# Stacked query and key parts loaded as long rows, the maxima's band copied heads outermost, and expert units moved to other places of the schedule

## The chip, the cores and the metric

The kernel runs on one core of one Trainium2 chip. The metric is the device time of one launch in microseconds (us), the median of several runs. The core has five engines that run their own instruction streams and meet in semaphores: TensorE (PE, with its weight loads shown as PEld), VectorE (DVE), ScalarE (ACT), GpSimd (POOL) and SyncE (SP), whose queue issues the DMAs here. Sixteen DMA engines move the bytes.

## The reference, cut to what matters

Eight samples go through one block, one after the other: a token mixer and a text embedding give 384 rows of 256, then attention with relative positions, then eight gated experts.

```python
h = concat([L0_tok(x), W_E[x_txt] * sqrt(256)], axis=1)      # (8, 384, 256)
# attention: 16 heads of 16, band of 9 relative positions (|s - t| <= 4)
q = (ln(h) @ Wq + bq) * 0.25;  k = ln(h) @ Wk + bk;  v = ln(h) @ Wv + bv
w = q @ k.T + rel_to_abs(q @ rel_k.T)                          # per head, 384 x 384
p = softmax(w)
h = h + (p @ v + abs_to_rel(p) @ rel_v) @ Wo + bo
# experts: e_out = (silu(x @ Wg) * (x @ Wu)) @ Wd per expert, weighted by a router
h = h + einsum('bte,betd->btd', weights(ln(h)), e_out)
```

## The kernel before, in words

**Staging.** `rounds` gives every engine the same list of steps from `schedule`: one round with attention of sample 0 alone, a loop of seven rounds (`Fori(1, NB)`) with attention of sample b and the experts of sample b - 1, and a last one with the experts of sample 7. An engine does of each step what its own block defines, so the order of steps is fixed by hand.

**Expert units.** The experts of a sample are 48 units of TensorE work: per expert two `gate`, two `up` (six matmuls of 384 columns each, in split precision) and `down` parts 0 and 1 (eight and four recorded matmuls). Each is followed by work of DVE (`hidden`, `accumulate`) or ACT (`silu`). `fill(n)` puts the next n units behind a step. The tables FILL_MIX, FILL_MAXIMA, FILL_NEGATE and FILL_OUT say how many: before, 31 units lie in the mixer and projections, 20 of them after `project_v`, 5 between the maxima, 2 after `negate` and 10 in the output part.

**Queries and keys.** `project_qk` computes q and k transposed: two blocks of 128 columns (m = 0, 1), partition = column within the block, 384 rows along the free axis. Each is split into three bf16 parts, `parts[0..5]`. SP writes each part to HBM (`part_out`, L533), in rows of 768 bytes of `d_parts[n]`, and `stack` (L538) reads them back, six DMAs for `q_st` and six for `k_st`: each fills 16 partitions (the 16 columns of a head) with 16 heads of 384 bf16. Six such groups of 16 partitions stand above each other, so one matmul over the partitions adds the products of the parts. Both `part_out` and `stack` write or read 192 KB per DMA.

**The band.** `project_rel` computes the relative logits; SP writes them askew to `d_band_t` (L549), reads the band back into `band_t` (L567, 128 partitions, bf16, window outer and head inner), and does the same in float32 for `bands` (L571, L580). All of these stand in SP's queue in this order: parts, `q_st` zero rows (L559), six loads of `q_st`, six of `k_st`, the load of `band_t`, three writes of `d_band_s`, two loads of `bands`.

**Maxima.** 24 items per sample, each of two tiles of 128 rows: a matmul `q_st` by `k_st` of 384 columns (L746), and one of the identity by `band_t[rows, i, w0:w1, h]` of 132 or 136 columns (L754), which reads one element in 16. Two pairs of PSUM banks take turns. DVE reduces both tiles of an item at once (`maxima`, L1168). Item 0 waits for all stacks and for `band_t`; item n waits for the reduction of item n - 2. After 12 and 24 items `negate` turns the maxima and SP takes them through HBM to rows 96 and 97 of `q_st`. Then `attend` computes scores anew, DVE adds `bands` (L1189), ACT takes exp (L999), POOL cuts windows (L1432).

**Start.** SP issues 9, 4 and 30 small loads (groups 0 to 2, L473), the zeroing of three HBM tensors (L493 to L504), then the first expert weights (L509). `prepare` (DVE, L1118 to L1131) waits for all of group 2, stands behind the sums of sample 0's mixer in DVE's order, and makes `rel_k` and others; ACT's and TensorE's first `project_qk` wait for the semaphore `consts`.

## Time and profile before

| | |
|---|---|
| median of 3 runs | 1387.92 us (1380.27 to 1393.97) |
| the profiled execution | 1391.63 us, span 1389.6 us |
| busy: PE, PEld, DVE | 1160.2, 811.2, 751.2 us |
| busy: ACT, POOL | 370.3, 234.4 us |
| granted TensorE clock, mean | 0.907 of full speed |
| DMA | 89.59 MB, mean 64 GB/s |

The span is the time from the first to the last instruction that the profile shows. Busy time is the sum over an engine's instructions, so an engine can be 83% busy and still be waited for only in parts. One round of the loop takes some 161 us. The stages below are those of the third round, whose stacks are issued from 389.5 us.

### The profile page before, as it was taken

What the parts mean: (1) busy time and instruction counts of PE and PEld (TensorE: products, weight loads), DVE (VectorE), ACT (ScalarE), POOL (GpSimd) and SP (SyncE); (2) the same over time, 40 slices, a digit from 0 to 9 for tenths busy, and PEclk for the clock granted to TensorE, in tenths of its full rate; (3) what the DMA queues carried; (4) which work ended last, traced back from release to release, by engine and by line L of the source; (5) the groups of instructions that cost most, each with busy time, mean ns of one, the idle gap of its engine ahead of it and who ended that gap; (6) DMA issues with size and microseconds to landing.
All of it is one profiled execution on the core that took longest, in us unless ns stands there. A gap on an engine that the chain in (4) does not pass through costs nothing.

```text
span 1389.6 us, 16995 instructions
## 1 busy us (share of the span) xinstructions
PE 1160.2 (83%) x5732; PEld 811.2 (58%) x5732; DVE 751.2 (54%) x1579; ACT 370.3 (27%) x599; POOL 234.4 (17%) x258
## 2 busy tenths in 40 slices
PE   5447699878898898988899788987889888997798
PEld 4212378426784377735785267843777357852588
DVE  6337264763548545573556635475455735466333
ACT  1214212062222522043220622115120432206111
POOL 5404120040200302022200402004020212004000
PEclk9667789988899989999899989999899998999889
DMA  6691207302092102901055020921029010650200
GB/s 210 159 199 62 43 5 128 86 1 59 0 161 52 35 23 57 155 1 35 23 96 116 5 54 0 162 51 35 23 51 160 1 35 23 100 112 1 46 0 12
DMA packets 126985, 89.59 MB, mean 64 GB/s; under 512 B 67991, under 2 KB 116504, under 8 KB 126522
## 3 DMA queue, kind: packets, MB, share of 16 engines
q1 hardware_dynamic: 126552, 88.05, 31.4%
q0 software_dynamic: 384, 1.05, 0.3%
q14 instruction: 38, 0.31, 0.1%
q8 instruction: 11, 0.18, 0.1%
HBM read 60.36 MB, written 28.71 MB: 64 GB/s over the span
## 4 chain that ended last, share of the span: by engine, by line
PE 31%; issue 28%; DVE 15%; DMA 12%; SPq 5%; ACT 5%; POOL 2%; POOLq 0%; DVEq 0%; ACTq 0%
DMA scratch<-d_band_t 9%; PE S L881 7%; PE S L754 4%; PE S L902 4%; DVE S L1189 4%; PE S L746 4%; SPq L538 4%; PE S L809 4%; ACT scratch L999 3%; DVE maxima L1168 3%; PE S L710 3%; PE S L794 2%; DMA txt_row<-in_L_txt_W_E,txt_idx 1%; PE S L627 1%; DMA w_d<-in_L_ffn_Wu 1%
## 5 line engine op out<-in xcount | busy, mean ns | idle before, releaser
L1168 DVE TENSOR_REDUCE maxima<-S 128x2 f32<-128x768 f32 x192 | 176.0, 953 | 82.1 <-PE S L754 80.6
L1432 POOL TENSOR_TENSOR bands<-scratch,one 64x432 f32<-64x432 f32 x128 | 119.5, 934 | 585.8 <-ACT scratch L999 580.7
L902 PE MATMUL S<-w_d,hT 128*128 128x256 f32 x768 | 198.6, 412 | 8.1 <-DVE hT L1306 8.1
L902 PEld LDWEIGHTS S<-w_d,hT 128*128 128x128 f32 x768 | 158.6, 210 | 34.1 <-issue 10.8
L746 PE MATMUL S<-k_st,q_st 128*128 128x384 bf16 x384 | 137.1, 357 | 49.1 <-DMA scratch<-d_band_t 34.7
L1189 DVE TENSOR_TENSOR S<-S,bands 64x144 f32<-64x144 f32 x384 | 154.3, 402 | 43.9 <-PE S L794 34.2
L999 ACT ACTIVATE scratch<-S 128x768 f32<-128x768 f32 x192 | 155.6, 811 | 56.5 <-DVE S L1189 49.1
L1037 ACT ACTIVATE silu<-S 128x384 f32<-128x384 f32 x128 | 62.9, 491 | 396.4 <-PE S L881 309.9
L754 PE MATMUL S<-scratch,ident_b 128*128 128x132 bf16 (+1 forms) x384 | 154.5, 402 | 0.0
L1306 DVE TENSOR_TENSOR hT<-silu,S 128x384 f32<-128x384 f32 x128 | 70.6, 552 | 117.9 <-PE S L881 115.7
L794 PE MATMUL S<-q_st,k_st 128*128 128x384 bf16 x384 | 93.2, 342 | 36.4 <-ACT scratch L999 34.8
L809 PE MATMUL S<-scratch,v_one 128*17 128x384 f32 x768 | 90.9, 569 | 27.5 <-ACT scratch L999 27.4
L746 PEld LDWEIGHTS S<-k_st,q_st 128*128 128x128 bf16 x384 | 38.5, 100 | 117.1 <-DVE maxima L1168 58.8
L1318 DVE SCALAR_TENSOR_TENSOR res<-S,wgt,res 128x256 f32<-128x256 f32 x168 | 75.5, 479 | 50.0 <-PE S L902 49.6
L794 PEld LDWEIGHTS S<-q_st,k_st 128*128 128x128 bf16 x384 | 25.6, 99 | 121.8 <-ACT scratch L999 92.5
L881 PE MATMUL S<-x_hi,wu_hi 128*128 128x384 f32 x256 | 75.5, 377 | 14.3 <-DVE hT L1306 14.0
L881 PE MATMUL S<-x_hi,wg_hi 128*128 128x384 f32 x256 | 80.3, 396 | 0.0
L627 PE MATMUL S<-ident,scratch 128*128 128x128 f32 x196 | 35.6, 330 | 52.0 <-DVE scratch L1079 30.1
L1349 POOL TENSOR_TENSOR rstd<-mv,eps 128x3 f32<-128x3 f32 (+1 forms) x24 | 4.6, 193 | 387.1 <-DVE mv L1073 387.1
L881 PE MATMUL S<-x_hi,wu_lo 128*128 128x384 f32 x256 | 68.3, 349 | 0.0
L881 PE MATMUL S<-x_lo,wu_hi 128*128 128x384 f32 x256 | 68.3, 349 | 0.0
L881 PE MATMUL S<-x_lo,wg_hi 128*128 128x384 f32 x256 | 67.2, 344 | 0.0
(159 smaller groups left out, 1578.4 us busy)
## 6 DMA issues: line engine op xcount, KB each, us to landing
bands<-d_band_s SPq DMA_DIRECT2D x16, 864.0 KB, 8.8
scratch<-d_band_t SPq DMA_DIRECT2D x8, 1632.0 KB, 16.9
d_parts<-scratch SPq DMA_DIRECT2D x48, 192.0 KB, 2.0
q_st<-d_parts SPq DMA_DIRECT2D x48, 192.0 KB
k_st<-d_parts SPq DMA_DIRECT2D x48, 192.0 KB
d_band_w<-bands SPq DMA_DIRECT2D x32, 240.0 KB, 3.8
out<-scratch SPq DMA_DIRECT2D x8, 384.0 KB, 2.7
x_in<-in_x SPq DMA_DIRECT2D x8, 256.0 KB, 3.7
```

Of the source, the lines that this page charges most:

```text
L746: pe.matmul(S[:, bank, PAD:PAD + T], q_st[:, h, i * P:(i + 1) * P], k_st[:, h, :], start=True, stop=False, skip_group_check=True)
L754: mm = pe.matmul(S[rows, bank, at + w0:at + w1], ident_b[rows, rows], band_t[rows, i, w0:w1, h], start=False, stop=True, skip_group_check= ...
L794: mm = pe.matmul(S[:, 2 * (n % 3) + l, PAD:PAD + T], k_st[:, h, i * P:(i + 1) * P], q_st[:, h, :], start=True, stop=True)
L809: mm = pe.matmul(S[32 * l:32 * l + VC, 6 + g % 2, 0:T], v_one[:, i, h, :], p_t[:, h % PTS, i, :], start=(i == 0), stop=(i == TT - 1), skip ...
L881: mm = pe.matmul(dst[:, 0:T], ws[:, e, k, m * P:(m + 1) * P], xs[:, k, :], start=(j == 0), stop=(j == 3 * KT - 1))
L902: mm = pe.matmul(D[:, i // 2, (i % 2) * E:(i % 2 + 1) * E], hT[:, (FT * e + m) % 3, i * P:(i + 1) * P], w_d[:, e, m, :], start=(m == 0), s ...
L999: nc.scalar.activation(dst, S[:, c0:c0 + 2, PAD:PAD + T], ACT.Exp).then_inc(exp_done.sem, 1)
L1168: dve.tensor_reduce(dst, S[:, c0:c0 + 2, PAD:PAD + T], AX, ALU.max).then_inc(max_done.sem, 1)
L1189: dve.tensor_tensor(win, win, band, ALU.add).then_inc(sc_add.sem, 1)
L1306: dve.tensor_tensor(hT[:, n % 3], silu[:], U[:, 0:T], ALU.mult).then_inc(h_done.sem, 1)
L1318: dve.scalar_tensor_tensor((out_st if last else res)[:, i], D[:, i // 2, (i % 2) * E:(i % 2 + 1) * E], wgt[:, i, e:e + 1], res[:, i], ALU. ...
L1432: nc.gpsimd.tensor_tensor(bands[rows, :, :, 2 * pair:2 * pair + 2].rearrange("p i w h -> p h i w"), win, one[rows].unsqueeze(2).unsqueeze( ...
```

## The change

The columns of Wq and Wk, and their biases, are reordered on chip so that a partition holds (d, group of heads) rather than (head, d). A part is then written to HBM as it lies on chip, in rows of 1536 bytes, and a stack DMA reads for each of its 16 partitions one run of 12,288 bytes. ScalarE copies `band_t` two heads at a time into `band_h`, heads outermost, and the identity matmuls read 132 neighbouring elements. The biases and `emb_rel_k` are loaded by 16 small DMAs each. The unit tables are changed: `project_v` 20 to 9, maxima 5 to 12, `negate` 2 to 3, output part 10 to 13.

```diff
...
 EPS = 1e-5
 ITEMS = AH * TT // 2
 WINS = P // BL
-N_LOADS = (9, 4, 13 + P // AD + NJ)
+N_LOADS = (9, 4, 10 + 3 * AD + NJ)
 N_ZERO = 8
-N_CONSTS = 8
+N_CONSTS = 12
 FILL_MIX = [("residual", 0), ("mix_in", 0), ("turn_x2", 0), ("mix_sums", 0), ("router", 1),
             ("mix_out", 0), ("router_zone", 1), ("mix_norm", 1), ("router_rank", 2),
             ("norm_stats", 2), ("router_pick", 1), ("turn_norm", 2), ("project_qk", 0),
-            ("project_rel", 1), ("project_v", 20)]
-FILL_MAXIMA = [0, 0, 0, 1, 0, 0, 0, 1, 0, 0, 0, 1, 0, 0, 0, 1, 0, 0, 0, 1, 0, 0, 0, 0]
-FILL_NEGATE = 2
-FILL_OUT = [("turn_outputs", 6), ("turn_weights", 2), ("rel_values", 2), ("turn_attn", 0)]
+            ("project_rel", 1), ("project_v", 9)]
+FILL_MAXIMA = [0, 1] * 12
+FILL_NEGATE = 3
+FILL_OUT = [("turn_outputs", 7), ("turn_weights", 2), ("rel_values", 3), ("turn_attn", 1)]
 R_DIST = 4
 ZONE_LO = float(np.float32(0.5 - np.log(4.0 / 3.0)))
 ZONE_HI = 0.5
...
         ident = sb("ident", [P, P])
         ident_b = sb("ident_b", [P, P], BF16)
-        head_of_row = sb("head_of_row", [P, KT, AH])
         head_of_rel = sb("head_of_rel", [P, AH])
         earlier = sb("earlier", [P, NE, NE])
         wkv = sb("wkv", [F + 1, 2 * F])
...
         emb_k_rows = zone(7640, NJ)
+        row_head, w_in = zone(7700, AH // KT), zone(6528, 2, KT, E)
         emb_v_rows0, emb_v_rows1 = zone(7656, AD), zone(7672, AD)
         rel_log_b = Z[:, 4272:4272 + TT * RJ // 2].bitcast(BF16).rearrange("p (i r) -> p i r", i=TT)
         BAND_AT = ZF - TT * ROWB // 2
         band_t = Z[:, BAND_AT:ZF].bitcast(BF16).rearrange("p (i w h) -> p i w h", i=TT, h=AH)
+        band_h = Z[:, 0:TT * ROWB // 2].bitcast(BF16).rearrange("p (i h w) -> p i h w", i=TT, h=AH)
+
...
         REL_TILES = ((0, S[:, 0, 0:E]), (1, S[:, 2, 0:E]), (2, O[:, 0:E]))
-        d_parts = nc.dram_tensor("d_parts", [6, E, T], BF16, kind="Internal").ap()
+        d_parts = nc.dram_tensor("d_parts", [6, P, KT, T], BF16, kind="Internal").ap()
         d_zero = nc.dram_tensor("d_zero", [2, AH, T], BF16, kind="Internal").ap()
         d_neg = nc.dram_tensor("d_neg", [2, 2, AH // 2, T], BF16, kind="Internal").ap()
         d_band_t = nc.dram_tensor("d_band_t", [T * ROWB], BF16, kind="Internal").ap()
...
         mask_float, wb_masked, ew_exp = sem("mask_float"), sem("wb_masked"), sem("ew_exp")
         ew_turned, ew_ready, resid_ready = sem("ew_turned"), sem("ew_ready"), sem("resid_ready")
         temp_inverse, wr_high, consts = sem("temp_inverse"), sem("wr_high"), sem("consts")
+        row_mask = sem("row_mask")
         gu_high, gu_low, pool_consts = sem("gu_high"), sem("gu_low"), sem("pool_consts")
         x_loaded = sig("x_loaded", 1, 16)
         idx_loaded = sig("idx_loaded", 1, 16)
...
         stacked = sig("stacked", 2 * SLOTS + 1, 16)
         rel_t_out, rel_s_out = sig("rel_t_out", P // BT, 16), sig("rel_s_out", TT, 16)
         band_t_in, band_s_in = sig("band_t_in", 1, 16), sig("band_s_in", WINS, 16)
+        band_turned = sig("band_turned", AH // 2)
         max_pe = sig("max_pe", ITEMS)
         max_done = sig("max_done", ITEMS)
         neg_pe, neg_act, neg_dve = sig("neg_pe", 2), sig("neg_act", 2), sig("neg_dve", 2)
...
                 (ln_g[:], a["L0_tok_ln_g"].partition_broadcast(P)),
                 (ln_b[:], a["L0_tok_ln_b"].partition_broadcast(P)),
             ], [
-                (head_of_row[:], a["head_of_row"]), (head_of_rel[:], a["head_of_rel"]),
+                (head_of_rel[:], a["head_of_rel"]),
                 (earlier[:], a["earlier"]),
-                (bq4[:], a["L0_attn_bq"].rearrange("(k p) -> p k", p=P)),
-                (bk1[:], a["L0_attn_bk"].rearrange("(k p) -> p k", p=P)),
-                (w_q[:], a["L0_attn_Wq"].rearrange("(k p) n -> p k n", p=P)),
-                (w_k[:], a["L0_attn_Wk"].rearrange("(k p) n -> p k n", p=P)),
+                (w_in[:, 0], a["L0_attn_Wq"].rearrange("(k p) n -> p k n", p=P)),
+                (w_in[:, 1], a["L0_attn_Wk"].rearrange("(k p) n -> p k n", p=P)),
                 (w_v[:], a["L0_attn_Wv"].rearrange("(k p) n -> p k n", p=P)),
                 (w_o[:], a["L0_attn_Wo"].rearrange("(k p) n -> p k n", p=P)),
                 (bv_all[:], a["L0_attn_bv"].partition_broadcast(P)),
...
             ]]
             emb_v = a["L0_attn_emb_rel_v"]
-            for r in range(P // AD):
-                groups[2].append((emb_k_rows[AD * r:AD * (r + 1)],
-                                  a["L0_attn_emb_rel_k"].rearrange("o j d -> d (o j)")))
+            G8 = P // AD
+            for d in range(AD):
+                rows = slice(d * G8, (d + 1) * G8)
+                groups[2] += [
+                    (emb_k_rows[rows], dram(a["L0_attn_emb_rel_k"], d, (0, G8), (AD, NJ))),
+                    (bq4[rows], dram(a["L0_attn_bq"], d, (KT * AD, G8), (AD, KT))),
+                    (bk1[rows], dram(a["L0_attn_bk"], d, (KT * AD, G8), (AD, KT)))]
             for j in range(NJ):
                 rows = slice(AH * j, AH * (j + 1)) if j < P // AH else slice(0, AH)
                 at = emb_v_rows0 if j < P // AH else emb_v_rows1
...
                 def part_out(n, done, k, out):
                     sp.wait_ge(done.sem, done.at(b, k))
-                    sp.dma_start(d_parts[n].rearrange("(m p) t -> p m t", p=P), parts[n]
+                    sp.dma_start(d_parts[n], parts[n]
                                  ).then_inc(out.sem, 16)
                 def stack(st, base, order):
                     for n in range(SLOTS):
                         sp.dma_start(
-                            st[AD * n:AD * (n + 1)],
-                            d_parts[base + order[n]].rearrange("(h d) t -> d h t", d=AD)
+                            st[AD * n:AD * (n + 1)].rearrange("p h t -> p (h t)"),
+                            d_parts[base + order[n]].rearrange("(d g) m t -> d (g m t)", d=AD)
                         ).then_inc(stacked.sem, 16)
                 part_out(0, proj_act, 3, q_out)
...
                     if not later(b):
                         pe.wait_ge(pool_consts, 8)
                     pe.wait_ge(stacked.sem, stacked.at(b, 2 * SLOTS + 1))
-                    pe.wait_ge(band_t_in.sem, band_t_in.at(b, 1))
-
                     pe.wait_ge(v_done.sem, v_done.at(b, TT))
                     pe.wait_ge(proj_act.sem, proj_act.at(b, 9))
+                if n % 3 == 0:
+                    pe.wait_ge(band_turned.sem, band_turned.at(b, n // 3 + 1))
                 if n >= 2:
                     pe.wait_ge(max_done.sem, max_done.at(b, n - 1))
                 for l, (h, i) in enumerate(tiles_of(n)):
...
                         w0, w1 = (WIN if first else 0), (WB - WIN if last else WB)
                         at = PAD + i * P + c * BT - WIN
                         mm = pe.matmul(S[rows, bank, at + w0:at + w1], ident_b[rows, rows],
-                                       band_t[rows, i, w0:w1, h],
+                                       band_h[rows, i, h, w0:w1],
                                        start=False, stop=True, skip_group_check=True)
                 mm.then_inc(max_pe.sem, 1)
...
                 act.wait_ge(proj_act.sem, proj_act.at(b, 9))
                 nc.scalar.activation(rel_log_b, rel_log, ACT.Copy).then_inc(proj_act.sem, 1)
+            def maxima(b, n):
+
+                if n == 0:
+                    act.wait_ge(band_t_in.sem, band_t_in.at(b, 1))
+                ahead = {0: (0, 1), ITEMS - 3: ()}
+                for pair in ahead.get(n, (n // 3 + 1,) if n % 3 == 0 else ()):
+                    heads = slice(2 * pair, 2 * pair + 2)
+                    nc.scalar.activation(band_h[:, :, heads], band_t[:, :, :, heads].rearrange("p i w h -> p i h w"),
+                                         ACT.Copy).then_inc(band_turned.sem, 1)
+
             def weights(b):
                 for n in range(4):
...
                 nc.scalar.activation(silu[:], G[:, 0:T], ACT.Silu).then_inc(silu_done.sem, 1)
             rounds(act, {"mix_in": mix_in, "prepare": prepare, "turn_norm": turn_norm,
-                         "project_qk": project_qk, "project_rel": project_rel, "weights": weights,
+                         "project_qk": project_qk, "project_rel": project_rel, "maxima": maxima, "weights": weights,
                          "negate": negate, "attend": attend, "copy": copy, "turn_weights": turn_weights,
                          "turn_attn": turn_attn, "turn_x2": turn_x2, "router": router, "gate": gate})
...
             def prepare(b):
                 dve.wait_ge(loaded[2], 16 * N_LOADS[2])
+                dve.tensor_tensor(row_head, head_of_rel[:, 0:AH // KT], head_of_rel[:, AH // KT:AH], ALU.add
+                                  ).then_inc(row_mask, 1)
+                dve.memset(rel_k[:], 0.0).then_inc(row_mask, 1)
+                dve.wait_ge(row_mask, 2)
                 for m in range(KT):
-                    dve.tensor_tensor(rel_k[:, m], emb_k_rows.unsqueeze(2).broadcast_to([P, NJ, AH]),
-                                      head_of_row[:, m].unsqueeze(1).broadcast_to([P, NJ, AH]), ALU.mult
+                    dve.tensor_tensor(rel_k[:, m].rearrange("p j (g m) -> p m j g", m=KT)[:, m],
+                                      emb_k_rows.unsqueeze(2).broadcast_to([P, NJ, AH // KT]),
+                                      row_head.unsqueeze(1).broadcast_to([P, NJ, AH // KT]), ALU.mult
                                       ).then_inc(consts, 1)
+                for n, w in enumerate((w_q, w_k)):
+                    for k in range(KT):
+                        dve.tensor_copy(w[:, k].rearrange("p (m d g) -> p m d g", m=KT, d=AD),
+                                        w_in[:, n, k].rearrange("p (g m d) -> p m d g", m=KT, d=AD)
+                                        ).then_inc(consts, 1)
                 for dst, rows, n in ((rel_v0, emb_v_rows0, P), (rel_v1, emb_v_rows1, RJ - P)):
                     dve.tensor_tensor(dst[:], rows[0:n].unsqueeze(1).broadcast_to([n, AH, AD]),
                                       head_of_rel[0:n].unsqueeze(2).broadcast_to([n, AH, AD]), ALU.mult
```

## Rows read from the trace of the kernel before

**Rows 1.** The page's chain that ended last, by line

```profile
DMA scratch<-d_band_t 9%; PE S L881 7%; PE S L754 4%; PE S L902 4%; DVE S L1189 4%; PE S L746 4%; SPq L538 4%; PE S L809 4%; ACT scratch L999 3%; DVE maxima L1168 3%; PE S L710 3%; PE S L794 2%; DMA txt_row<-in_L_txt_W_E,txt_idx 1%; PE S L627 1%; DMA w_d<-in_L_ffn_Wu 1%
```

**Rows 2.** The same chain in order of time: start, us, what

```profile
388.63 0.36 SPq L533
...
396.87 16.91 DMA scratch<-d_band_t
...
422.52 1.05 PE S L881 x6
...
443.22 2.59 PE S L902 x12
```

**Rows 3.** Windows of transfers: engines' busy time, clock, DMA share, GB/s

```profile
387.50:388.00 0.50, 0.50 (x4) 0.45 (x3) 0.47 (x2) 0.00 (x0) 0.00 (x0) 1.00 1.00 307
392.00:409.00 17.00, 17.00 (x92) 16.26 (x91) 6.25 (x13) 2.46 (x5) 0.00 (x0) 1.00 1.16 131
393.25:393.50 0.25, 0.25 (x3) 0.25 (x2) 0.25 (x2) 0.00 (x0) 0.00 (x0) 1.00 1.12 108
394.00:394.25 0.25, 0.25 (x3) 0.25 (x2) 0.00 (x0) 0.00 (x0) 0.00 (x0) 1.00 1.40 191
...
395.50:395.75 0.25, 0.25 (x3) 0.25 (x3) 0.25 (x1) 0.00 (x0) 0.00 (x0) 1.00 1.35 194
410.50:412.00 1.50, 1.50 (x10) 1.37 (x9) 0.55 (x1) 0.02 (x1) 0.00 (x0) 1.00 1.04 418
474.50:476.50 2.00, 1.39 (x13) 0.55 (x6) 0.00 (x0) 1.07 (x2) 0.00 (x0) 0.84 1.01 200
420.00:422.00 2.00, 1.76 (x10) 0.60 (x8) 1.79 (x3) 0.00 (x0) 0.00 (x0) 1.00 1.03 200
```

**Rows 4.** TensorE in order of time, before and after its wait

```profile
399.67 0.71 PE L881 MATMUL S<-x_hi,wg_hi 128*128 128x384 f32 x2
...
414.09 0.33 PE L746 MATMUL S<-k_st,q_st 128*128 128x384 bf16 x1 [1.32 <-DMA scratch<-d_band_t]
...
414.26 0.40 PE L754 MATMUL S<-scratch,ident_b 128*128 128x132 bf16 x1
...
414.48 0.34 PE L746 MATMUL S<-k_st,q_st 128*128 128x384 bf16 x1
```

**Rows 5.** The same window view of the maxima stage and of the output part

```profile
414.09:442.70 28.61, 26.28 (x127) 13.96 (x127) 23.92 (x30) 1.46 (x3) 0.00 (x0) 1.00 0.33 66
...
475.35:498.26 22.91, 19.91 (x96) 16.12 (x97) 7.74 (x19) 5.09 (x10) 0.00 (x0) 0.93 0.25 44
```

**Rows 6.** Groups by line in one maxima stage: busy us, mean ns, idle before

```profile
L1168 DVE TENSOR_REDUCE maxima<-S 128x2 f32<-128x768 f32 x24 | 21.9, 952 | 7.1 <-PE S L754 7.1
```

**Rows 7.** Groups by line over the whole span

```profile
L1318 DVE SCALAR_TENSOR_TENSOR res<-S,wgt,res 128x256 f32<-128x256 f32 x168 | 75.5, 479 | 50.0 <-PE S L902 49.6
L1306 DVE TENSOR_TENSOR hT<-silu,S 128x384 f32<-128x384 f32 x128 | 70.6, 552 | 117.9 <-PE S L881 115.7 <-DVE scratch L1279 1.3
...
L959 ACT ACTIVATE scratch<-scratch 128x768 bf16<-128x768 f32 x16 | 13.5, 843 | 0.5
```

**Rows 8.** Windows of the clock, the first round's and a later one's

```profile
63.00:84.00 21.00, 0.03 (x1) 0.06 (x2) 0.00 (x0) 0.00 (x0) 5.84 (x2) 0.50 1.14 185
84.00:92.50 8.50, 8.50 (x30) 3.25 (x31) 6.07 (x7) 0.00 (x0) 0.00 (x0) 0.50 0.70 129
...
471.50:475.25 3.75, 3.73 (x24) 0.94 (x24) 0.00 (x0) 0.00 (x0) 1.87 (x2) 0.54 0.25 52
```

**Rows 9.** Loads at the start, and who waits for them

```profile
18.38 4.13 SPq L473 DMA_DIRECT2D scratch<-in_L_attn_emb_rel_v  x9
...
23.67 0.20 ACT L937 ACTIVATE bq<-bq 128x2 f32<-128x2 f32 x1 [6.44 <-DMA scratch<-in_L_attn_emb_rel_v]
...
36.81 0.51 DVE L1118 TENSOR_TENSOR rel_k<-scratch,head_of_row 128x144 f32<-128x144 f32 x2
```


## The prediction

> **What bounds the kernel now.** I read the page first. Its chain by line gives the wait for `scratch<-d_band_t`, the load of the maxima's band, the largest share, 9% [rows 1]. The chain in order of time says why: the last part leaves at 388.63, the twelve stacks follow, the load of `band_t` is issued at 396.87 and takes 16.91 us although it is one DMA [rows 2]. It stands behind the stacks in the same rings. In the windows the stacks fill the time from 392 to 409 at 131 GB/s, and the band itself then runs at 418 [rows 3]. TensorE works through its 20 units meanwhile and idles 1.32 us before item 0 at 414.09 [rows 4]. So before this point two things are nearly equal: 20 units of TensorE's work, and the stacks. In the maxima stage (28.61 us) PE is busy 26.28 and DVE 23.92 us [rows 5]; in the output part PE is busy 19.91 of 22.91 us [rows 5]. TensorE's work is the bound of the loop, and moving units pays only where the place they leave shrinks by as much.
>
> **Do longer rows make the stacks faster?** This decides the sum. Within one stack the windows show a plateau of 108 GB/s, with a peak of 191 to 194 each time the next stack begins, at 394.0 and again at 395.5 [rows 3]: one stack in 1.5 us, twelve in 18. Parts are written from 128 partitions in the same 768-byte rows at 307 GB/s, so that row length is not what holds the stacks at a third of this. Transfers with long rows but fewer partitions are slow too: the loads of `bands` (64 partitions, rows of 4608 bytes) run at 200 GB/s, the stores of windows (32 partitions each, rows of 2560 bytes) at 200, `band_t` on 128 partitions at 418 [rows 3]. The rate follows the partitions that a transfer spans, and a stack still spans 16. I therefore take 1.5 us for a stack as before. Bounds: 1.8 us, if the peaks at the seams vanish (196,608 bytes at 108 GB/s), and 1.25 us, if the seams grow to twice their share; for twelve that is +3.7 and -3.0 us a round.
>
> The Trainium skill, SBUF — State Buffer, section "Door 1: The DMA port swizzle", speaks against this change: 16 partitions reach 4 of 16 ports, and it gives 104 GB/s for a 1 MiB transfer on partitions 0 to 15, whose rows are long. The trace agrees within a stack (108 GB/s). By the page's figure a stack would take an estimated 1.89 us, and the sum would be some 37 us higher over eight rounds.
>
> **Units leaving `project_v`.** Nine units instead of 20 follow `project_v`. In the trace the ninth ends at 399.64, where the next gate begins at 399.67 [rows 4]. With the stacks as slow as before the band still lands at 413.8, so PE idles some 15 us there: nothing is gained.
>
> **The copy to `band_h`.** PE no longer waits for the load but for ACT's copy of the first head pair: 3*2*136 = 816 elements. ACT copies 768 to bf16 in 0.843 us [rows 7], so 0.90 us, plus a semaphore: item 0 starts 1.1 us later (0.9 to 2.0, if reading one element in 16 doubles it). The other seven copies run ahead on an ACT that is busy 1.46 of 28.61 us [rows 5]; what queues behind them is `silu`, with slack. Cost zero.
>
> **The maxima stage.** Now a tile is a matmul of 384 columns and one of the identity. They start 0.17 and 0.22 us apart (414.09, 414.26, 414.48 [rows 4]): the short one takes longer than the long one. With neighbouring elements it should take between its share at the other's rate (0.06) and no gain (0.22); I take 0.10, near the long one's rate but with a weight load of its own. An item is then 2*(0.18+0.10) = 0.56 us of PE instead of 0.80. A gate or up takes 1.05 us, both down parts together 2.59 [rows 2], so a unit is (4*1.05+2.59)/6 = 1.13 us. Two items and their unit: 1.12+1.13 = 2.25 us. DVE: 21.9/24 = 0.91 us an item [rows 6], and per six units two `hidden` (0.55) and three `accumulate` (0.48) [rows 7], 0.42 a unit: 1.82+0.42 = 2.24. Both engines are full; twelve such pairs take 27.0, and the transposes, the last reduction and semaphores 1.6: 28.6 us at full clock, as now, with seven units more. That is what the contiguous band buys: 24*0.24 = 5.8 us of PE, about five units.
>
> But the stage now starts after 15 us of idle. In the first round PE idles from 63 to 84 and the granted clock is 0.50; it stays there for 8.5 us of work, 84.0 to 92.5, and in a later place for 3.75 us of dense work [rows 8]. The maxima with units are dense, so nearer the second: 5 us at 1.2 instead of 2.4 GHz, 2.5 us lost (1.9 to 4.3). The stage takes 31.1 us: +2.5.
>
> **Units arriving elsewhere.** `negate` holds gate, up, gate (3*1.05) instead of both down parts (2.59): +0.6. The output part gets three units more, up and both down parts: 1.05+2.59 = 3.6 us. PE idles 22.91-19.91 = 3.0 us there now [rows 5], in the waits for the output's copies, the windows' way through HBM and the expert tail; I count 2.3 of it as filled (a unit behind a wait fills it, one that overshoots delays the chain): +1.3. Together +1.9 a round (0.9 to 3.5).
>
> **The start.** Group 2 grows from 30 loads to 10+48+9 = 67. Nine small ones are issued in 4.13 us [rows 9], 0.46 each, so 37 more take 17.0 us on SP, ahead of the zeroing and the expert weights. The last load ends its issue at 22.5 and ACT passes at 23.67 [rows 9]; now at 40.7. DVE reaches `prepare` at 36.81 [rows 9], so 13 of the 17 us are hidden by the first mixer and 3.9 are not. DVE adds a mask sum, a memset and four copies of 256 columns, each at most the 0.48 of an `accumulate` of that width: 2.1 us, all in the chain that leads to the first norm. Start: +6.0 (4.5 to 8).
>
> **The sum.** Seven rounds of the loop: 7*(0+1.1+2.5+1.9) = 38.5. First round: no units; its end waits for expert weights whose loads stand in SP's queue behind the band, so neither copy nor item counts: 0. Start 6.0. Last round unchanged. 1391.63+44.5 = 1436; against the median, 3.7 us below the profiled execution, **1432 us**. Its own range: stacks -24 to +30, clock -4 to +13, identity matmul up to +30 (no gain) or -5, the rest -10 to +15: these hardly come together, 1400 to 1475.
>
> **Rivals.**
> (a) *Long rows do free the stacks.* If 768-byte reads, not the 16 partitions, set 131 GB/s, a stack takes 0.47 to 0.64 us (196,608 bytes at 418 or 307 GB/s [rows 3]), and twelve some 7 instead of 18: 11 us less. The band lands near 402.8, three to four us after the ninth unit. A round changes by -11+1.1+0+1.9 = -8.0 with hardly any clock lost: -56, first round and start -11+6: 1326 to 1335, **1329 us**. For it: no other transfer here reads 768-byte rows from HBM into 16 partitions, and the mean of 131 GB/s lies above the plateau. Against: the plateau itself and the 32- and 64-partition rows. It is faster from the point where a round saves more than the 5.5 us it costs plus its share of the start, at stacks under 0.96 us.
> (b) *Engines run on.* With one run of 12,288 bytes per engine and stack, engines that finish early write the next stack's partitions, and the 194 GB/s of the seams [rows 3] becomes the mean: 1.01 us a stack, -5.9 a round. Then 7*(-5.9+5.5) = -3, first round and start about 0: **1385 us**, no change.
> (c) *The identity matmul gains nothing.* 0.22 as before: PE 2.73 us per pair of items, +5.8 a round more on the forecast, 1472. It lies in the forecast's range.
>
> **Chances.** Forecast with (c) 0.64, (b) 0.12, (a) 0.24. Under 1% (14 us) this kernel's runs hardly tell from no change. Slower by more: 0.60, from the forecast less its low tail; within 1%: 0.14; faster: 0.26, (a) and a part of (b). Range: the forecast's own up to 1475, (b), and half of (a): 1332 to 1475.
>
> **What would show it.** Right: windows of the stacks again near 108 GB/s within one and 1.5 us apart; PE idle some 15 us before item 0 and clock 0.50 in the first microseconds of the maxima; short matmuls under 0.12 us apart; `prepare` waiting for a load near 40 us. Wrong: a band load that lands under 10 us after its issue and stacks over 250 GB/s. The forecast falls with its first step, the rate of a stack; everything else in it is worth some 10 us.

## The result, and the profile after

The changed kernel takes 1471.62 us (median of 4 runs, 1469.70 to 1473.85) beside 1390.16 us for the kernel before on the same chip (4 runs). The ratio is 1.0618, with a 95% interval of 1.0572 to 1.0663: 81 us slower. The profiled execution took 1469.7 us, its span is 1467.9 us against 1389.6 before, +78.3.

The page of the changed kernel, its busy times and the chain by line:

```profile
span 1467.9 us, 17186 instructions
...
PE 1086.0 (74%) x5732; PEld 786.7 (54%) x5732; DVE 747.9 (51%) x1585; ACT 473.1 (32%) x663; POOL 234.1 (16%) x258
...
DMA scratch<-d_band_t 9%; PE S L887 7%; DVE maxima L1194 4%; PE S L908 3%; PE S L815 3%; ACT scratch L1015 3%; DVE S L1215 3%; SPq L479 3%; PE S L716 3%; SPq L544 3%; ACT scratch L985 3%; PE S L800 2%; PE S L752 2%; PE S L633 1%; DMA txt_row<-in_L_txt_W_E,txt_idx 1%
...
L985 ACT ACTIVATE scratch<-scratch 128x816 bf16<-128x816 bf16 x64 | 106.3, 1703 | 121.5 <-DMA scratch<-d_band_t 121.5
```

TensorE has 74 us less to do (1160.2 before) and the kernel is longer all the same. The band's load still leads the chain [rows 1]; two lines are new on it, SP's small loads (L479) and ACT's copies (L985), 3% each.

**Where the 78.3 us lie.** A round begins for this count when SP issues its first part (`part_out`). The marks, from SP's queue in order of time, split the span:

| stretch | before, us | after, us | difference | forecast |
|---|---|---|---|---|
| start to the first part | 54.37 | 69.57 | +15.2 | +6.0 |
| first part of round 0 to that of round 1 | 161.84 | 173.96 | +12.1 | 0 |
| the next six, mean of one | 162.8 | 170.8 | +8.0, six times | +5.5 |
| from the last such mark to the end | 196.7 | 199.7 | +3.0 | +5.5 |

15.2 + 12.1 + 6*8.0 + 3.0 = 78.3. Single rounds scatter: the six of the kernel before lie between 160.1 and 167.2 us (the third round's 161 among them), those after between 170.2 and 171.9. The 8.0 lie far outside this scatter, while one or two us between the means of two kernels may be scatter.

**The start.** SP's loads and DVE's first steps behind them, in order of time (start, us, what, and the idle time before it with its releaser):

```profile
23.32 0.68 SPq L479 DMA_DIRECT2D bq<-in_L_attn_bq  x1
24.04 0.67 SPq L479 DMA_DIRECT2D bk<-in_L_attn_bk  x1
24.75 0.46 SPq L479 DMA_DIRECT2D scratch<-in_L_attn_emb_rel_k  x1
...
44.53 4.03 SPq L479 DMA_DIRECT2D scratch<-in_L_attn_emb_rel_v  x9
...
49.66 0.17 DVE L1133 TENSOR_TENSOR scratch<-head_of_rel 128x8 f32<-128x8 f32 x1 [12.77 <-DMA scratch<-in_L_attn_emb_rel_v]
49.83 0.30 DVE L1135 MEMSET rel_k<- 128x288 f32 x1
...
50.46 0.65 DVE L1144 COPY w_q<-scratch 128x256 f32<-128x256 f32 x2
51.03 0.65 DVE L1144 COPY w_k<-scratch 128x256 f32<-128x256 f32 x2
```

The pattern of three loads repeats 16 times. A load of `emb_rel_k` costs 0.46 us, as the small loads did before [rows 9], but each slice of a bias costs 0.68, or 0.72 from one issue to the next. The nine loads of `emb_rel_v` end at 48.56 instead of 22.51, and DVE waits 12.77 us for them.

**The first round.** ACT, TensorE and DVE in order of time:

```profile
117.34 1.91 ACT L993 ACTIVATE wu_hi<-w_d 128x2048 fp32r<-128x2048 f32 x1 [40.25 <-DMA w_d<-in_L_ffn_Wu]
120.28 1.91 ACT L993 ACTIVATE wu_hi<-w_d 128x2048 fp32r<-128x2048 f32 x1 [1.03 <-DMA w_d<-in_L_ffn_Wu]
122.09 9.53 ACT L985 ACTIVATE scratch<-scratch 128x816 bf16<-128x816 bf16 x6
123.90 0.48 PE L752 MATMUL S<-k_st,q_st 128*128 128x384 bf16 x1 [48.98 <-ACT scratch L985]
...
124.96 1.82 DVE L1194 TENSOR_REDUCE maxima<-S 128x2 f32<-128x768 f32 x2 [49.03 <-PE S L760]
```

ACT takes its steps in program order. The cast of the expert weights (`weights`, before `maxima` in the schedule) waits 40.25 us for the load of `Wu`, and the new copies stand behind it. Item 0 of the maxima starts at 123.90; before, it started at 84.0 [rows 8], since it needed no step of ACT behind the cast. Counted from the round's own first part, that is 54.3 us instead of 29.6.

**The stage that the forecast reads, third round.** The chain in order of time:

```profile
425.33 20.11 DMA scratch<-d_band_t
445.46 1.67 ACT scratch L985
447.18 0.50 PE S L752
...
456.27 1.76 ACT scratch L985
458.15 0.33 PE S L752
```

SP's queue there, in order of time:

```profile
417.96 1.31 SPq L539 DMA_DIRECT2D d_parts<-scratch  x2
419.42 0.25 SPq L565 DMA_DIRECT2D q_st<-d_zero  x1
419.80 2.63 SPq L544 DMA_DIRECT2D q_st<-d_parts  x6
422.48 2.73 SPq L544 DMA_DIRECT2D k_st<-d_parts  x6
425.33 0.38 SPq L573 DMA_DIRECT2D scratch<-d_band_t  x1
```

Windows of the same stage, columns as in [rows 3]:

```profile
421.50:439.50 18.00, 8.84 (x46) 7.94 (x44) 3.41 (x8) 0.98 (x2) 0.00 (x0) 0.84 1.03 121
430.00:433.00 3.00, 0.34 (x2) 0.00 (x0) 0.39 (x1) 0.00 (x0) 0.00 (x0) 1.00 0.94 111
447.18:479.66 32.48, 28.25 (x171) 20.70 (x171) 26.78 (x36) 13.69 (x12) 0.00 (x0) 0.94 0.27 55
447.18:451.00 3.82, 3.82 (x15) 2.86 (x16) 2.21 (x3) 1.51 (x1) 0.00 (x0) 0.53 0.45 94
451.00:452.00 1.00, 1.00 (x11) 0.77 (x9) 0.48 (x1) 0.94 (x2) 0.00 (x0) 1.00 1.01 203
```

The stacks with their rows of 12,288 bytes run at 121 GB/s, where those of 768 bytes ran at 131 [rows 3]. The load of the band lands 20.11 us after its issue (16.91 before [rows 2]) and 26.5 us after the last part was ready; before it was 25.1. TensorE has done its nine units long before; its instructions in order of time:

```profile
447.18 0.50 PE L752 MATMUL S<-k_st,q_st 128*128 128x384 bf16 x1 [16.84 <-ACT scratch L985]
447.48 0.32 PE L760 MATMUL S<-scratch,ident_b 128*128 128x132 bf16 x1
447.59 0.53 PE L752 MATMUL S<-k_st,q_st 128*128 128x384 bf16 x1
...
451.04 0.22 PE L760 MATMUL S<-scratch,ident_b 128*128 128x132 bf16 x1
451.10 0.33 PE L752 MATMUL S<-k_st,q_st 128*128 128x384 bf16 x1
```

It idles 16.84 us and runs at half clock until 451 (0.53), then at full. At full clock a long matmul (384 columns) follows a short one (the identity's, 132 columns) after 0.06 us (451.04 to 451.10), where it took 0.22 us before [rows 4]. The maxima stage takes 32.48 us (28.61 before [rows 5]). At its end the turn of the maxima has to wait for DVE's three `accumulate` steps of the unit just ahead of it (they read the PSUM bank that it writes); DVE and TensorE in order of time:

```profile
478.35 1.26 DVE L1344 SCALAR_TENSOR_TENSOR res<-S,wgt,res 128x256 f32<-128x256 f32 x3
479.66 0.49 PE L633 MATMUL S<-ident,maxima 128*8 128x128 f32 x3 [1.73 <-DVE res L1344]
```

### The profile page after: what moved, and what is told of

Same layout as the page of the kernel before. It is cut to its first block, busy times and chain, and to the rows that moved or that the text cites. A ratio compares the mean times of both kernels' runs of the same rounds, so it can differ in the third digit from the quotient of the medians.

```text
span 1467.9 us, 17186 instructions
## 1 busy us (share of the span) xinstructions
PE 1086.0 (74%) x5732; PEld 786.7 (54%) x5732; DVE 747.9 (51%) x1585; ACT 473.1 (32%) x663; POOL 234.1 (16%) x258
## 4 chain that ended last, share of the span: by engine, by line
issue 30%; PE 24%; DVE 15%; DMA 13%; ACT 8%; SPq 7%; POOL 2%; POOLq 0%; DVEq 0%; ACTq 0%
DMA scratch<-d_band_t 9%; PE S L887 7%; DVE maxima L1194 4%; PE S L908 3%; PE S L815 3%; ACT scratch L1015 3%; DVE S L1215 3%; SPq L479 3%; PE S L716 3%; SPq L544 3%; ACT scratch L985 3%; PE S L800 2%; PE S L752 2%; PE S L633 1%; DMA txt_row<-in_L_txt_W_E,txt_idx 1%
## 5 line engine op out<-in xcount | busy, mean ns | idle before, releaser
L752 PE MATMUL S<-k_st,q_st 128*128 128x384 bf16 x384 | 108.7, 349 | 175.0 <-ACT scratch L985 166.5
L908 PE MATMUL S<-w_d,hT 128*128 128x256 f32 x768 | 181.9, 382 | 6.2 <-DVE hT L1332 6.2
L908 PEld LDWEIGHTS S<-w_d,hT 128*128 128x128 f32 x768 | 141.3, 190 | 26.1 <-issue 7.6
L985 ACT ACTIVATE scratch<-scratch 128x816 bf16<-128x816 bf16 x64 | 106.3, 1703 | 121.5 <-DMA scratch<-d_band_t 121.5
L815 PE MATMUL S<-scratch,v_one 128*17 128x384 f32 x768 | 85.7, 536 | 25.6 <-ACT scratch L1015 25.2
L760 PE MATMUL S<-scratch,ident_b 128*128 128x132 bf16 (+1 forms) x384 | 88.8, 232 | 0.0
L887 PE MATMUL S<-x_lo,wg_hi 128*128 128x384 f32 x256 | 71.2, 362 | 0.0
L633 PEld LDWEIGHTS S<-ident,scratch 128*128 128x128 f32 x196 | 27.9, 169 | 78.2 <-DVE scratch L1095 53.8
L887 PE MATMUL S<-x_hi,wg_lo 128*128 128x384 f32 x256 | 69.6, 355 | 0.0
```

The costliest lines, as they stand in the source:

```text
L633: return pe.transpose(dst, src, ident[0:rows, 0:rows])
L752: pe.matmul(S[:, bank, PAD:PAD + T], q_st[:, h, i * P:(i + 1) * P], k_st[:, h, :], start=True, stop=False, skip_group_check=True)
L760: mm = pe.matmul(S[rows, bank, at + w0:at + w1], ident_b[rows, rows], band_h[rows, i, h, w0:w1], start=False, stop=True, skip_group_check= ...
L815: mm = pe.matmul(S[32 * l:32 * l + VC, 6 + g % 2, 0:T], v_one[:, i, h, :], p_t[:, h % PTS, i, :], start=(i == 0), stop=(i == TT - 1), skip ...
L887: mm = pe.matmul(dst[:, 0:T], ws[:, e, k, m * P:(m + 1) * P], xs[:, k, :], start=(j == 0), stop=(j == 3 * KT - 1))
L908: mm = pe.matmul(D[:, i // 2, (i % 2) * E:(i % 2 + 1) * E], hT[:, (FT * e + m) % 3, i * P:(i + 1) * P], w_d[:, e, m, :], start=(m == 0), s ...
```

## The experiments

Theory A is the forecast's, with the three costs that the trace of the changed kernel added to it: slow stacks on 16 partitions with an empty TensorE above them, SP's many small loads, and ACT's order in round 0. Its rivals are named in the expectations. The kernel before ran on each chip too, at medians of 1383.0 (the first four experiments), 1385.2 (the next four) and 1387.5 us (the last four), so kernels are compared by their ratios, and by the marks of their traces. "A round" below is the mean of the six stretches between marks. In the diffs "..." stands for lines left out.

### The unit tables of before (e1_old_tables)

```diff
-            ("project_rel", 1), ("project_v", 9)]
-FILL_MAXIMA = [0, 1] * 12
-FILL_NEGATE = 3
-FILL_OUT = [("turn_outputs", 7), ("turn_weights", 2), ("rel_values", 3), ("turn_attn", 1)]
+            ("project_rel", 1), ("project_v", 20)]
+FILL_MAXIMA = [0, 0, 0, 1, 0, 0, 0, 1, 0, 0, 0, 1, 0, 0, 0, 1, 0, 0, 0, 1, 0, 0, 0, 0]
+FILL_NEGATE = 2
+FILL_OUT = [("turn_outputs", 6), ("turn_weights", 2), ("rel_values", 2), ("turn_attn", 0)]
```

> The changed kernel with the four unit tables of the kernel before. Theory A (the stacks are as slow as before, so the 11 units left a hole in which TensorE idles and its clock falls): the hole closes, the maxima stage is bound by VectorE with only 5 units in it (24*0.91 plus 2.0 plus 1.5 = 25.4 us instead of 32.5), later stages give 2 us back, the band lands as before: a round loses 9 us, 7*9 = 63, about 1408 us. Rival B (the copies to band_h, 1.70 us each, hold the round up wherever the units are): a round loses 3 us or less, 1450 us or more.

Measured: 1408.99 us, ratio 1.0165 (1.0111 to 1.0219). A round takes 161.0 us, 9.8 less than in the changed kernel. TensorE idles 2.17 us before item 0 of the third round instead of 16.84. So the places of the units make all of the loop's loss that can be told from the 162.8 before. The start and round 0 keep their losses (first parts at 69.64 and 245.36).

### One load for each of the three arrays (e2_few_loads)

```diff
-            for d in range(AD):
-                rows = slice(d * G8, (d + 1) * G8)
-                groups[2] += [
-                    (emb_k_rows[rows], dram(a["L0_attn_emb_rel_k"], d, (0, G8), (AD, NJ))),
-                    (bq4[rows], dram(a["L0_attn_bq"], d, (KT * AD, G8), (AD, KT))),
-                    (bk1[rows], dram(a["L0_attn_bk"], d, (KT * AD, G8), (AD, KT)))]
+            groups[2] += [(emb_k_rows, a["emb_k_rows"]), (bq4[:], a["bq_rows"]), (bk1[:], a["bk_rows"])]
...
```

The three arrays are laid out in rows on the host, before the launch.

> The changed kernel with the two biases and emb_rel_k laid out in rows beforehand and loaded by one DMA each, 3 instead of 48. Theory A (SP's issue of the small loads holds up the first projections): project_qk of the first round moves from 62.5 us to 50 or less, 13 to 15 us off the whole, 1457 us. Rival B (the first round ends with the expert weights in any case, so a later start is absorbed): no change, 1471 us.

Measured: 1456.33 us, ratio 1.0526 (1.0496 to 1.0557). The first part leaves at 56.66 us instead of 69.57: 12.9 of the start's 15.2 us are the 45 loads. Of the 2.3 us that stay, DVE's added steps in `prepare` are 1.5 (it takes 3.1 us instead of 1.6), and the first projection takes 0.8 more: its eight matmuls by `w_q` take 5.46 us, all in a stretch at half clock, and took 4.68, the last part of them at full clock.

### Round 0's copies ahead of the cast of Wu (e3_copies_first)

```diff
             def maxima(b, n):
+                if not later(b):
+                    return
...
                 for n in range(4):
+                    if n == 2:
+                        act.wait_ge(band_t_in.sem, band_t_in.at(b, 1))
+                        for pair in range(AH // 2):
+                            heads = slice(2 * pair, 2 * pair + 2)
+                            nc.scalar.activation(band_h[:, :, heads], ...
```

> The changed kernel with ScalarE's eight copies of the first round ahead of its casts of the Wu halves, instead of behind them. Theory A (in the first round the maxima wait for copies queued behind casts that wait for weights): the maxima start about 105 instead of 124 us and end before the weights are ready; attend follows the landing of Wu by 18 instead of 28 us, 10 us off, 1461 us. Rival B (SP's negate stands behind the weights, so the maxima's place does not matter): no change, 1471 us.

Measured: 1458.05 us, ratio 1.0534 (1.0504 to 1.0565). ACT and TensorE in order of time, round 0:

```profile
101.48 12.59 ACT L996 ACTIVATE scratch<-scratch 128x816 bf16<-128x816 bf16 x8 [24.46 <-DMA scratch<-d_band_t]
103.29 0.48 PE L752 MATMUL S<-k_st,q_st 128*128 128x384 bf16 x1 [29.06 <-ACT scratch L996]
...
118.11 1.91 ACT L1001 ACTIVATE wu_hi<-w_d 128x2048 fp32r<-128x2048 f32 x1 [4.04 <-DMA w_d<-in_L_ffn_Wu]
```

The same copies, the same wait for the band, and in round 0 only the order changed: item 0 starts 20 us earlier, the cast still finds its data late (4.04 us), and round 0 takes 162.0 us, as before the change. So this order makes the 12.1 us of round 0.

### The strided read kept, no copy (e4_no_copy)

```diff
-                if n % 3 == 0:
-                    pe.wait_ge(band_turned.sem, band_turned.at(b, n // 3 + 1))
...
-                                       band_h[rows, i, h, w0:w1],
+                                       band_t[rows, i, w0:w1, h],
...
```

TensorE waits for the band's load again, and ACT's copies are taken out.

> The changed kernel without the copies: the identity matmuls read one element in 16 of band_t again, with the new tables. Theory A (the contiguous band makes room on TensorE, the copy costs a start and the first round): start of the maxima 1.7 us earlier, two items and a unit 2.73 instead of 2.25 us of TensorE, stage 34.5 instead of 32.5 us, first round 10 us less: 7*0.3-10, about 1463 us. Rival B (the copies are the main cost of a round): 3 us or more off each round, 1440 us or less. Rival C (TensorE is the bound of the stage): 5 us or more on each, 1495 us or more.

Measured: 1482.16 us, ratio 1.0701 (1.0670 to 1.0732), between theory A and rival C: the loss in a round is ten times what A gave. Round 0 gets 12.4 us shorter, the other rounds 3.4 us longer each (174.2). Groups by line: the identity's matmuls are back at their length of before.

```profile
L759 PE MATMUL S<-scratch,ident_b 128*128 128x132 bf16 (+1 forms) x384 | 154.8, 403 | 0.0
```

So with 12 units between the maxima the contiguous band is worth 3.4 us a round net of its copy. It is the part of the change that earns something. Counted from item 0 to the last reduction the stage takes 36.0 us here and 31.2 with `band_h`, 4.8 us of the 5.8 of TensorE that the prediction worked out; the first copy takes 1.4 of them back.

### The three fixes together (e5_three_fixes)

Old tables, few loads and copies first, in one kernel; the long rows and the contiguous band stay.

> The changed kernel with old unit tables, few start loads and the first round's copies ahead of the casts, together. Theory A (the three losses lie in different stretches and add up): 1471.6-62.6-15.3-13.6 = 1380 us, level with the kernel before or up to 1% faster, since long rows and band_h cost and gain little by themselves. Rival B (they overlap: the first round waits for the expert weights in any case): 1395 us or more.

Measured: 1383.17 us (10 runs), ratio 0.9986 (0.9949 to 1.0024). The three costs add up, and what is left of the change, as a whole, is worth nothing that can be told. A round takes 161.5 us (162.8 before). That hides two effects of opposite sign, which e8 below separates.

### One load on 96 partitions for each stack (e6_wide)

`part_out` writes a part once for every slot that uses it, into `d_stack`, and one DMA per stack reads all six slots. Its rows have the same 12,288 bytes and all loads together move the same bytes; one spans 96 partitions instead of 16, and there are two instead of twelve.

```diff
-                    for n in range(SLOTS):
-                        sp.dma_start(
-                            st[AD * n:AD * (n + 1)].rearrange("p h t -> p (h t)"),
-                            d_parts[base + order[n]].rearrange("(d g) m t -> d (g m t)", d=AD)
-                        ).then_inc(stacked.sem, 16)
+                    sp.dma_start(
+                        st[0:KST].rearrange("p h t -> p (h t)"),
+                        d_stack[base // 3].rearrange("s (d g) m t -> (s d) (g m t)", d=AD)
+                    ).then_inc(stacked.sem, 16)
...
```

> The changed kernel, but each part is written to HBM once for each slot that uses it, and q_st and k_st are each loaded by one DMA over 96 partitions instead of six over 16; rows of 12,288 bytes and all bytes read stay the same, written bytes double. Theory A (a stack's rate goes by the partitions that a transfer spans): the two loads take 4 to 5 us each instead of 18 together, the band lands 9 us earlier in each of 8 rounds, 72 us off, 1400 us. Rival B (something else holds the stacks at 131 GB/s, the reading side for one): no gain, 1475 us with the additional writes.

Measured: 1420.48 us, ratio 1.0229 (1.0155 to 1.0303). Windows of the stacks in the third round:

```profile
413.00:415.00 2.00, 2.00 (x11) 1.77 (x10) 0.88 (x3) 0.00 (x0) 0.00 (x0) 1.00 1.03 255
415.00:417.00 2.00, 2.00 (x13) 2.00 (x12) 0.58 (x2) 0.49 (x1) 0.00 (x0) 1.00 1.02 258
```

The chain in order of time behind them:

```profile
414.02 14.95 DMA scratch<-d_band_t
429.00 1.67 ACT scratch L986
430.71 0.50 PE S L753
```

The rate doubles. It is not the number of loads that held it down: in both traces the DMA engines are busy all through (DMA share 1.03 here, and 1.03 at 121 GB/s above), and a packet of 12,288 bytes takes 0.81 us instead of 1.56 in the mean of the 194 of this stage. That the loads also read other places of HBM was not tried by itself. From the issue of the first stack (412.20) to the landing of the band it takes 16.8 us instead of 25.6, nearly the 9 us less that were expected. The size fell short all the same, 54 us by the ratios and 49 by the spans where 72 were expected. In the mean of six rounds it is 17.1 instead of 24.8 us, and the first stack is issued 1.0 us later, behind six more writes of parts. So the band lands 6.7 us earlier after a round's first part, and a round gives back 7.0 us (163.8). Round 0 gives back 2.6 only, as its item 0 still stands behind the cast of `Wu`. The Trainium skill, SBUF — State Buffer, section "Door 1: The DMA port swizzle", lets the rate follow the ports that the partitions of one transfer reach. The runs agree: 16 partitions stay at 121 to 131 GB/s with either row, 96 give 255.

### The same with the start and round 0 mended (e7_wide_fixes)

e6 with few loads and copies first.

> The same 96-partition loads with few start loads and the first round's copies ahead of the casts, new unit tables. Theory A: the gains of those two fixes (15.3 and 13.6 us) add to the wide loads' 72: 1371 us, faster than the kernel before. Rival B (without the slow stacks in front, the first round's end is set by the expert weights alone, and the fixes there no longer count in full): 1385 us.

Measured: 1391.10 us (10 runs), ratio 1.0027 (0.9999 to 1.0055). Against e6 that is 29 us less, both mends in full; the miss against the expectation (1371 us) is e6's. A round still takes 163.7 us, with 9.5 us of idle ahead of item 0 in the third: nine units are too few even for the fast stacks, as e9 below shows.

### The long rows alone (e8_rows_alone)

Old tables, few loads, no copy: of the change only the order of columns and rows, with DVE's steps for it at the start, is left.

> Long rows alone: old unit tables, no copy to band_h, few start loads. Theory A (the length of the rows does not matter on 16 partitions): stacks again 1.5 us apart, the whole within 0.5% of the kernel before, 1383 to 1390 us. Rival B (long rows free the stacks, and only the other edits hide it): the band lands 10 us earlier in the first round and TensorE no longer waits for it elsewhere, 1365 us.

Measured: 1403.42 us, ratio 1.0117 (1.0043 to 1.0192). The window of the stacks in the third round:

```profile
391.50:410.00 18.50, 18.50 (x99) 17.57 (x98) 6.81 (x14) 2.45 (x5) 0.00 (x0) 1.00 1.02 131
```

131 GB/s, as before. Long rows free nothing. The kernel is slower than theory A allowed (1383 to 1390 us): all four runs (1398.18 to 1406.57) lie above every run of the kernel before on this chip (up to 1396.23). The trace, of the fastest of the four, shows the 2.3 us of e2 at the start and about 1 us more a round (163.9 against 162.8); TensorE's waits for the band, over eight rounds, are 40.2 us, and were 34.7 before. Where the rest of the 18 us between the medians lies, no run shows.

Beside e5, measured on the same chip, this kernel is 20 us slower, and the only differences are the copy to `band_h`, its place in round 0 and the contiguous read. So the contiguous band pays with the old tables too, 2.3 us a round by the marks (161.5 against 163.9), and in e5 it covers what the long rows and the start cost.

### Units in other places with the fast stacks (e9_wide_tables and e12_wide_tables2)

Both are e7 with tables of their own:

```diff
-            ("project_rel", 1), ("project_v", 9)]
-FILL_MAXIMA = [0, 1] * 12
-FILL_NEGATE = 3
-FILL_OUT = [("turn_outputs", 7), ("turn_weights", 2), ("rel_values", 3), ("turn_attn", 1)]
+            ("project_rel", 1), ("project_v", 15)]
+FILL_MAXIMA = [0, 0, 1] * 8
+FILL_NEGATE = 2
+FILL_OUT = [("turn_outputs", 7), ("turn_weights", 2), ("rel_values", 2), ("turn_attn", 1)]
...
```

The second has 13 units behind `project_v`, eight between the maxima in uneven steps, two at `negate` and 8, 3, 2 and 1 in the output part.

> The 96-partition loads with both fixes and unit tables fitted to the landing of the band: 15 units after project_v, one after every third item of the maxima (8), 2 after negate, 7, 2, 2 and 1 in the output part. Theory A (the loop is bound by TensorE once the hole is filled, and the maxima stage by VectorE with room for about one unit in three items): TensorE's hole of 6 to 7 us a round closes, the stage falls by 4 us, 5 us off a round, 1355 us, 2% under the kernel before. Rival B (VectorE's stage and the copies bind wherever the units lie): 1385 us.

> The same with 13 units after project_v, 8 in the maxima, 2 after negate, 8, 3, 2 and 1 in the output part. Theory A: two units of the hole are not used and lengthen the output part instead by 2.2 us a round: 1370 us. Rival B (the output part has room for them, in the waits for the windows' way through HBM): 1355 us, as the other table.

Measured: 1344.66 us, ratio 0.9680 (0.9630 to 0.9730), and 1374.04 us, ratio 0.9899 (0.9849 to 0.9948). The first is the best kernel of the study, 43 us under the one before (theory A said 1355 us). A round takes 157.1 us. The second table falls where its theory A put it (1370 us): with two units fewer in the hole and two more in the output part a round takes 162.2 us. From the third round of the first, TensorE in order of time:

```profile
396.29 0.34 PE L747 MATMUL S<-k_st,q_st 128*128 128x384 bf16 x1 [2.01 <-ACT scratch L981]
```

With 15 units the idle time before item 0 is 2.01 us, and the matmul there takes 0.34 us, its length at full clock. The clock isn't spared altogether: from 396.70 to 400.05 it is at 0.50. This is the exchange at which the change aims, here with the faster stack. Neither these tables with the slow stacks nor the old tables with the fast ones were run, so how much of the 43 us is the tables' and how much the stack's is not shown beyond e7: with the same stack, its tables cost 6.6 us a round more.

### The copy made short (e10_short_copy)

ACT copies 816 neighbouring elements of the band instead of one in 16; what it copies isn't the two heads' band.

```diff
-                    nc.scalar.activation(band_h[:, :, heads], band_t[:, :, :, heads].rearrange("p i w h -> p i h w"),
+                    nc.scalar.activation(band_h[:, :, heads], band_t[:, :, 0:WB // 8].rearrange("p i w h -> p i (w h)").rearrange("p i (x w) -> p i x w", x=2),
```

> The changed kernel whose copies to band_h read neighbouring elements instead of one in 16 (what they copy is then not the band; sizes and waits stay). Theory A (the 1.70 us of a copy come from reading one bf16 in 16, 32 bytes apart): 0.88 us a copy, item 0 starts 0.8 us earlier, the first round's end 0.8 us or more, PE's later waits for copies go: about 1 us a round, 1462 us. Rival B (a bf16 source or the four-dimensional pattern costs it, not the stride): 1.70 us a copy again and 1471 us.

Measured: 1455.82 us, ratio 1.0481 (1.0412 to 1.0550). The group of the copies:

```profile
L985 ACT ACTIVATE scratch<-scratch 128x816 bf16<-128x816 bf16 x64 | 53.2, 872 | 120.3 <-DMA scratch<-d_band_t 120.3
```

Each copy takes 872 instead of 1703 ns, and a round 168.4 instead of 170.8. Of these 2.4 us the first copy explains 0.8. TensorE's two waits a round for later copies are gone (one is at 456.27 above, where the copy stands behind a `silu`; they came to 0.8 us a round), but the stage from item 0 to the turn of its maxima gets only 0.3 us shorter. So the copies' length costs about 1.1 us a round, as theory A had it. The other 1.3 us, by which the kernel is faster than expected, lie in stretches without a copy, and nothing was tried on them.

### TensorE kept busy while the stacks load (e11_busy_hole)

80 matmuls more per round stand between the last unit and the wait for the stacks; item 0 writes over what they leave.

```diff
+                    if later(b):
+                        for _ in range(80):
+                            pe.matmul(S[:, 0, 0:T], wg_hi[:, 0, 0, 0:P], x2_hi[:, 0, :], start=True, stop=True)
```

> The changed kernel with 80 matmuls of 384 columns more in each loop round, in TensorE's wait between project_v's units and item 0, about 14 of its 17 us; their result is overwritten. Theory A (the idle stretch lowers the clock and the start of the maxima stage pays for it): the clock stays at 1.0 through item 0, the stage is 2 us shorter, 7*2 = 14 us off although work is added, 1457 us. Rival B (that stage is bound by VectorE and the copies even at the lower clock): 1471 us. Rival C (the added matmuls overrun the band's landing): 1480 us or more.

Measured: 1464.63 us, ratio 1.0559 (1.0492 to 1.0626). Windows of the third round:

```profile
427.00:447.00 20.00, 19.16 (x108) 18.40 (x108) 1.99 (x4) 2.73 (x3) 0.00 (x0) 1.00 0.98 173
447.00:451.00 4.00, 4.00 (x29) 3.10 (x28) 3.77 (x5) 3.32 (x3) 0.00 (x0) 1.00 0.61 138
```

Here the clock stays at 1.00 through the hole and the start of the maxima, and a round takes 169.0 us, 1.8 less. In the four rounds whose stage runs at full clock throughout, item 0 to the turn of the maxima takes 30.9 us, where it takes 32.2 to 32.8 in the changed kernel: the half clock costs the stage about 1.5 us, less than the 2.5 of the prediction. Over the whole span 5.5 us are left of this (1462.4 against 1467.9), where 14 were expected; the ratio's interval overlaps that of the changed kernel, so the times alone show no gain.

## Why the prediction was right in direction and too small

The forecast was 1432 us, the measured median 1471.62. It lies inside the range (up to 1475), near its edge. Against the span the forecast summed to +44.5 where +78.3 were measured. Of the 33.8 us between them 9.2 lie in the start, 12.1 in round 0, 15.0 in the six rounds between marks, and the last stretch gave 2.5 back.

**The rate of a stack: right.** "A stack still spans 16" decided the sum, and rivals (a) and (b) fell: 121 GB/s in the window above and 131 in e8, whose rows are long, and 255 in e6 with the same rows on 96 partitions. The loss that the bounds allowed (up to 3.7 us a round) stays small: the band lands 1.3 us later in the third round and 0.4 in the mean of six.

**Units leaving `project_v`: right.** Some 15 us of idle were forecast, 16.84 are there, and e1 took them away.

**The first round: the step that failed.** "Its end waits for expert weights ... so neither copy nor item counts: 0." This looked at the end of the round and not at ACT's own queue. The copy adds a wait of TensorE for ACT, and ACT was not free. The trace of the kernel before shows it, in ACT's order of time:

```profile
99.96 1.91 ACT L977 ACTIVATE wu_hi<-w_d 128x2048 fp32r<-128x2048 f32 x1 [38.35 <-DMA w_d<-in_L_ffn_Wu]
102.64 1.91 ACT L977 ACTIVATE wu_hi<-w_d 128x2048 fp32r<-128x2048 f32 x1 [0.77 <-DMA w_d<-in_L_ffn_Wu]
104.45 0.46 ACT L986 ACTIVATE neg_max<-S 8x384 bf16<-8x384 f32 x1
```

The turn of the first maxima (`negate`, L986) stood behind this cast already; the first twelve items did not, and ran while ACT waited. Now no item runs in this wait. Within the round item 0 slips by 24.7 us, about half of which the wait at `negate` had cost anyway, and 12.1 come through. e3 gives them back.

**The start: mis-sized.** The step has the right three parts. "Nine small ones are issued in 4.13 us ..., 0.46 each, so 37 more take 17.0": the last load's issue ends at 48.56, 26.0 us later than before instead of 17.0, since 32 of the 48 loads cost 0.68 us and not 0.46. Then 12.9 us were not hidden rather than 3.9 (e2). The 2.1 us for DVE's additions came out as 2.3 by luck: the additions are 1.5, and the 0.8 beside them are the first projection's, which the forecast did not count.

**The loop: right steps, mis-sized terms.** Means of the six rounds between marks, each stretch measured from the end of the one before:

| stretch of a round | before, us | after, us | difference | forecast |
|---|---|---|---|---|
| first part to the landing of the band | 30.52 | 30.95 | +0.4 | 0 |
| to item 0 | 0.33 | 1.74 | +1.4 | +1.1 |
| to the turn of the last maxima | 29.19 | 32.46 | +3.3 | +2.5 |
| to the first exp | 5.24 | 5.50 | +0.3 | +0.6 |
| to the last store of windows | 28.16 | 28.45 | +0.3 | 0 |
| to the output's store | 22.57 | 23.77 | +1.2 | +1.3 |
| to the next first part | 46.76 | 47.90 | +1.1 | 0 |

*The copy.* 0.90 us was taken, with 2.0 as the bound "if reading one element in 16 doubles it"; it does, 1.70. "The other seven copies ... Cost zero" is nearly right: TensorE waits 0.8 us a round for them, and with short copies the stage gets 0.3 us shorter (e10).

*The maxima stage.* The mechanism was right: the identity matmul became shorter than taken (0.06 us instead of 0.10), rival (c) is out, and the clock came back after 4 us, for which 5 were taken. The sizes agree in part by luck. At full clock 28.6 us were forecast and 30.9 are measured (e11). The forecast left out the three `accumulate` steps between the last reduction and the turn, 1.1 us (1.2 now, 0.1 before); 0.3 are the copies; the rest stays open. Against that the half clock cost 1.5 instead of 2.5. That it would be short because the maxima are "dense" does not follow from the rows: in the first round of the kernel before, TensorE was busy for all of the 8.50 us at half clock too [rows 8].

*Units elsewhere.* The output part loses what was forecast for its three units. The last 1.1 us lie between the output and the next round's parts, where no unit was moved. The granted clock differs there: in these six stretches TensorE was at 1.2 GHz for 15.4 us in the mean, and for 10.8 before. Windows of the third round, before and after:

```profile
497.60:544.31 46.71, 40.55 (x180) 34.05 (x181) 23.87 (x68) 10.90 (x22) 9.92 (x14) 0.89 0.06 17
537.09:585.64 48.55, 42.80 (x180) 36.08 (x181) 23.76 (x68) 9.55 (x20) 9.89 (x14) 0.82 0.05 17
```

The changed kernel's one round with less half clock there (6.8 us, its fifth) is also its shortest, 46.1 us. Why the clock falls more often there no run took apart.

## What to carry to other kernels

Before an engine gets a new step that others wait for, read what that engine is doing at this point in every round, the first above all: its program order is a queue, and one wait for a late load holds all behind it. Filling work may leave the place under a slow transfer only once the transfer is faster, and what made a load faster here was the number of partitions it spans, not the length of its rows. A small DMA is priced by the row of one of its own shape, and a copy by one of its own stride. A single round is not the loop: take the mean of several before a microsecond is explained.
